# A ninth 2 MB buffer in a two-batch convolution kernel: what it does to loads and stores

## The reference: what is computed

```python
xl1 = _bn_relu(_dwconv(x, w1), g1, b1)          # w1 covers the whole height
xl2 = _bn_relu(_dwconv(x, w2), g2, b2)          # w2 covers the whole width
dot_cb = jnp.einsum('bck,bck->cb', xl1[:, :, 0, :], xl2[:, :, :, 0])
num = dot_cb.reshape(b, c)
num = num @ lw1.T + lb1
num = num @ lw2.T + lb2
num = jax.nn.softmax(num, axis=1)
return x * num[:, :, None, None]                # inside: x is _gn(x); outside: _gn(x) + this
```

## Time and profile before

| | |
|---|---|
| median of 3 runs | 1786.57 us (1786.38 to 1789.39) |
| the profiled execution's own time | 1788.11 us |
| its span | 1786.4 us |
| moved by DMA | 728.07 MB, mean 408 GB/s over the span |
| VectorE busy | 933.8 us (52%) |
| ScalarE busy | 649.6 us (36%) |
| TensorE busy | 484.8 us (27%) |
| GpSimd busy | 318.1 us (18%) |

### The profile page before, as it was taken

How to read it: one execution, slowest core, us unless ns; L and a number is a source line. 1 busy time by engine, 2 the same in 40 slices (tenths; PEclk the granted TensorE clock), 3 DMA queues, 4 the chain that set the end, 5 groups by cost and what they waited for, 6 DMA issues and landing times.

```text
span 1786.4 us, 12512 instructions
## 1 busy us (share of the span) xinstructions
PE 484.8 (27%) x3214; PEld 163.5 (9%) x3214; DVE 933.8 (52%) x4046; ACT 649.6 (36%) x504; POOL 318.1 (18%) x409
## 2 busy tenths in 40 slices
PE   4588566642132322322322233440000000000000
PEld 1132122120000010100100010120000000000000
DVE  5899699933655654555565546963222222222221
ACT  4688587844444544543355345510000000000000
POOL 7678587820000000000000000010000000000000
PEclk8899788865666656656665666765555555555555
DMA  9997899959999999999999999999999999999999
GB/s 387 425 427 304 356 427 427 427 223 419 403 428 401 405 411 409 400 394 430 404 398 405 399 400 431 429 369 413 430 433 430 432 431 431 431 431 431 431 430 409
DMA packets 52425, 728.07 MB, mean 408 GB/s; under 512 B 6273, under 2 KB 6785, under 8 KB 8066
## 3 DMA queue, kind: packets, MB, share of 16 engines
q1 hardware_dynamic: 34210, 463.03, 61.7%
q10 hardware_dynamic: 18144, 264.25, 35.2%
HBM read 458.82 MB, written 268.44 MB: 407 GB/s over the span
## 4 chain that ended last, share of the span: by engine, by line
DMA 53%; another core or an unknown queue 26%; ACT 7%; DVE 6%; PE 4%; SPq 1%; issue 1%; POOL 1%; ACTq 0%; POOLq 0%; DVEq 0%
DMA xs<-in_x 40%; DMA out<-xs 12%; DVE mul_junk L829 4%; ACT sq_junk L650 4%; ACT xs L711 3%; PE ps_part L478 2%; DVE xs L907 1%; DMA z<-in_w 1%; SPq L307 1%; PE ps_l L571 0%; PE ps_m L584 0%; PE ps_l L559 0%; SPq L263 0%; SPq L255 0%
## 5 line engine op out<-in xcount | busy, mean ns | idle before, releaser
L829 DVE SCALAR_TENSOR_TENSOR mul_junk<-xs,ps_w 128x256 bf16<-128x256 f32 x1856 | 643.1, 417 | 317.3 <-DMA xs<-in_x 290.4
L650 ACT ACTIVATE sq_junk<-xs 128x4096 fp8e5<-128x4096 f32 x128 | 463.3, 3619 | 421.7 <-DMA xs<-in_x 405.9
L478 PE MATMUL ps_part<-xs,taps 128*32 128x512 f32 x2048 | 339.8, 824 | 658.2 <-DMA xs<-in_x 658.2
L907 DVE TENSOR_SCALAR xs<-xs,scale,shift 128x4096 f32<-128x4096 f32 x98 | 239.9, 2467 | 409.8 <-DMA xs<-in_x 409.2
L478 PEld LDWEIGHTS ps_part<-xs,taps 128*32 128x32 f32 x2048 | 91.0, 144 | 879.8 <-issue 866.0
L829 DVE DVE_READ_ACCUMULATOR mul_junk<-xs,ps_w 128x1 f32 x1856 | 153.3, 83 | 0.0
L396 POOL TENSOR_TENSOR rstd_b<-var,minus_half 128x2 f32<-128x2 f32 (+1 forms) x16 | 12.4, 774 | 717.8 <-DVE var L856 717.8
L370 POOL TENSOR_TENSOR prod<-xs,w_copy 128x768 f32<-128x768 f32 x64 | 116.4, 1825 | 79.8 <-DMA xs<-in_x 77.5
L711 ACT ACTIVATE xs<-xs,shift,scale 128x4096 f32<-128x4096 f32 x30 | 113.7, 3788 | 14.0 <-DVE scale L940 7.1
L376 POOL TENSOR_TENSOR prod<-prod 128x384 f32<-128x384 f32 x64 | 63.0, 1006 | 0.0
L380 POOL TENSOR_TENSOR prod<-prod 128x192 f32<-128x192 f32 x64 | 36.6, 594 | 0.0
(11 more groups left out here) (100 smaller groups left out, 280.6 us busy)
## 6 DMA issues: line engine op xcount, KB each, us to landing
xs<-in_x SPq DMA_DIRECT2D x216, 2048.0 KB, 19.8
out<-xs ACTq DMA_DIRECT2D x126, 2048.0 KB, 27.1
xs<-in_lw SPq DMA_DIRECT2D x2, 2048.0 KB, 20.8
out<-xs SPq DMA_DIRECT2D x2, 2048.0 KB, 10.9
w_c<-in_w_rows SPq DMA_DIRECT2D x1, 512.0 KB, 4.6
w_sb<-in_w SPq DMA_DIRECT2D x1, 512.0 KB, 9.7
z<-in_w SPq DMA_DIRECT2D x1, 512.0 KB, 23.7
affine_in<-in_g SPq DMA_DIRECT2D x2, 16.0 KB
```

The costliest lines, as they stand in the source:

```text
L478: last = nc.tensor.matmul(ps_part[g % 2][32 * a:32 * a + 32, :], taps[:, g // QG % 2, g % 2, hf * JH + j, :], xs[:, s[0]:s[1] + 1:s[1] - s ...
L650: nc.scalar.activation(sq_junk[:], xs[:, s, :], ACT.Square, accum_out=sq_sum[:, u % 2, u // 2, b:b + 1], saturate=False).then_inc(squared, 1)
L829: last = nc.vector.scalar_tensor_tensor(out=mul_junk[:, sets[0] % 2, j - first, :], in0=xs[:, s, j * W:(j + 1) * W], scalar=1.0, in1=ps_w2 ...
L907: return nc.vector.tensor_scalar(xs[:, s, :], xs[:, s, :], scale[:, b, g:g + 1], shift[:, b, g:g + 1], ALU.mult, ALU.add)
```

## The change

There are nine slots. The room comes from `taps`, which loses its second copy (its halves that hold plain ones are now written anew for the first two groups of every four), and from `mul_junk`, which becomes an 8-bit float tile. The ninth slot, number 8, is used for reloads together with 6 and 7 (`AHEAD = 3`), and at the end it holds one more `b = 1` part for stage 3 (`HELD = 5`), so stage 3 loads 59 parts instead of 60. The ring of three slots lasts to unit 18 instead of 14 (`RING3` 15 to 19).

```diff
-S = 8
+S = 9
-RING3 = 15
+RING3 = 19
 KEPT = 4
+HELD = 5
 REWORK = FIRST - KEPT
-LAST_ORDER = list(range(UNITS - KEPT, UNITS)) + list(range(UNITS - KEPT))
+AHEAD = 3
+LAST_ORDER = list(range(UNITS - HELD, UNITS)) + list(range(UNITS - HELD))
@@ def slot_of(u, b):
-    return 4 + u % 2 + 2 * (u >= UNITS - 2)
+    return 8 if u == UNITS - HELD else 4 + u % 2 + 2 * (u >= UNITS - 2)
 def rework_slot(r):
-    return 6 + r % 2
+    return (8, 6, 7)[r % AHEAD]
 def last_slot(i):
-    return (4 + i) % S
+    return (8 + i) % S if i < 1 or i % S == 0 else (3 + i % S) % 8
@@ tiles
-        taps = sb("taps", [P, 2, 2, JR, 2 * CG])
+        taps = sb("taps", [P, 2, JR, 2 * CG])
-        mul_junk = sb("mul_junk", [P, 2, SET, W], bf16)
+        mul_junk = sb("mul_junk", [P, 2, SET, W], mybir.dt.float8e5)
@@ SyncE
             def load_again(r):
                 s = rework_slot(r)
-                if r < 2:
-                    free_of_statistics(FIRST - 2 + r, 1)
-                else:
-                    sp.wait_ge(x_stored[s], written(s, ("re", r - 2)))
+                if r >= AHEAD:
+                    sp.wait_ge(x_stored[s], written(s, ("re", r - AHEAD)))
+                elif r:
+                    free_of_statistics(FIRST - 3 + r, 1)
...
+            load_again(0)
             load(FIRST, 1)
             load(FIRST + 1, 1)
-            load_again(0)
             load_again(1)
+            load_again(2)
...
-                if u - FIRST + 2 < REWORK:
-                    load_again(u - FIRST + 2)
+                if u - FIRST + AHEAD < REWORK:
+                    load_again(u - FIRST + AHEAD)
-            for i in range(KEPT, UNITS):
+            for i in range(HELD, UNITS):
@@ GpSimd
             def build(g):
                 qp = g // QG % 2
+                if g % QG < 2:
+                    nc.gpsimd.tensor_copy(taps[:, g % 2, :, CG * (1 - qp):CG * (2 - qp)],
+                                          own[:].unsqueeze(1).to_broadcast([P, JR, CG]))
                 nc.gpsimd.tensor_tensor(
-                    taps[:, qp, g % 2, :, CG * qp:CG * (qp + 1)], own[:].unsqueeze(1).to_broadcast([P, JR, CG]),
+                    taps[:, g % 2, :, CG * qp:CG * (qp + 1)], own[:].unsqueeze(1).to_broadcast([P, JR, CG]),
                     bc(w1_sb[:, g, :], CG), ALU.mult).then_inc(taps_ready, 1)
@@ ScalarE
-            rework(0)
-            rework(1)
+            for r in range(AHEAD):
+                rework(r)
...
-                    if b == 0 and u > FIRST and u - FIRST + 1 < REWORK:
-                        rework(u - FIRST + 1)
+                    if b == 0 and u > FIRST and u - FIRST - 1 + AHEAD < REWORK:
+                        rework(u - FIRST - 1 + AHEAD)
@@ VectorE, in multiply_rows
-                            out=mul_junk[:, sets[0] % 2, j - first, :], in0=xs[:, s, j * W:(j + 1) * W], scalar=1.0,
+                            out=mul_junk[:, sets[0] % 2, j - first, :], in0=xs[:, s, j * W:(j + 1) * W], scalar=1.0, saturate=False,
```

More of the change, by code:

```diff
@@ L71 @@
 for _i in range(UNITS):
-    if _i >= KEPT:
+    if _i >= HELD:
         LOADS[last_slot(_i)].append(("last", _i))
@@ L333, in build @@
                 qp = g // QG % 2
+                if g % QG < 2:
+                    nc.gpsimd.tensor_copy(taps[:, g % 2, :, CG * (1 - qp):CG * (2 - qp)],
+                                          own[:].unsqueeze(1).to_broadcast([P, JR, CG]))
                 nc.gpsimd.tensor_tensor(
-                    taps[:, qp, g % 2, :, CG * qp:CG * (qp + 1)], own[:].unsqueeze(1).to_broadcast([P, JR, CG]),
+                    taps[:, g % 2, :, CG * qp:CG * (qp + 1)], own[:].unsqueeze(1).to_broadcast([P, JR, CG]),
                     bc(w1_sb[:, g, :], CG), ALU.mult).then_inc(taps_ready, 1)
-            def plain(qp, i):
-                then_wait(nc.gpsimd.tensor_copy(
-                    taps[:, qp, i, :, CG * (1 - qp):CG * (2 - qp)], own[:].unsqueeze(1).to_broadcast([P, JR, CG])))
-            plain(0, 0)
             pool.wait_ge(w1_loaded, 16)
             build(0)
-            plain(0, 1)
             build(1)
@@ L418, in setup @@
                 if u == 0:
-                    for i in range(2):
-                        plain(1, i)
                     then_wait(nc.gpsimd.memset(minus_half[:], -0.5))
@@ L478, in convolve @@
                     last = nc.tensor.matmul(
-                        ps_part[g % 2][32 * a:32 * a + 32, :], taps[:, g // QG % 2, g % 2, hf * JH + j, :],
+                        ps_part[g % 2][32 * a:32 * a + 32, :], taps[:, g % 2, hf * JH + j, :],
                         xs[:, s[0]:s[1] + 1:s[1] - s[0], j * W:(j + 1) * W],
@@ L972, in _ @@
                 s = last_slot(i)
-                if i >= KEPT:
+                if i >= HELD:
                     dve.wait_ge(x_loaded[s], landed(s, ("last", i)))
```

## The result

The changed kernel takes 1745.93 us (median of 4 runs, 1745.46 to 1746.32) against 1787.98 us (4 runs, 1786.38 to 1789.44) for the kernel before in the same series: a ratio of 0.9765, 95% interval 0.9752 to 0.9777. That is 42.1 us or 2.35% faster. The forecast was 1736 with a range of 1724 to 1760, so the time lies inside the range, 9.9 us above the predicted value.

The account below looks back on a forecast made before the run. DMA transfers at a 431 GB/s ceiling were taken as the bound. Gains of 4.9 + 17.0 + 4.9 + 24 = 50.8 us left 1737.3 of the profiled 1788.1, 1735.8 as median: forecast 1736 us, range 1724 to 1760.

Parts of the forecast that it names:

- The frame: Whole kernel: transfers bound it; stretches below 431 GB/s lose about 99 us of the 1786.4 us span.
- the ring: Stage 1, 155 to 190 us: three slots to unit 18 remove the wait behind the copied bias, gaining 17.0 of 20.6 us.
- the third reload slot and its early reload: Stage 2 and the gap before it: gains of 24 and 4.9 us, 28.9 together.
- One held part more: Stage 3: one load fewer in a saturated stretch, 2.097 MB at 431 GB/s, gaining 4.9 us.
- The rival of the half-closed gap: Stage 1: unit 20's load is as late as the bias was, gain 9.7 instead of 17, 1743 us; chance 0.12.
- The ninth slot between the stages: End of stage 1: the first reload needs no wait and fills 4.9 us of the dead gap of 373 to 393.
- Three reload slots in stage 2: 450 to 1100 us: releases come about one unit earlier, reads do not run dry; 24 of 36.2 us gained, about 422 GB/s.
- The first rival: Stage 2 keeps its rate of 407 as the next wait stops SyncE as long; gain 0 to 10, 1755 us; chance 0.22.
- the full recovery: Stage 2 wins back all 36.2 us instead of 24, 1724 us; chance 0.08.
- End of stage 2: Unit 59's part waits for the last reload's store but is due two units later: unchanged, 0; 8.3 us stay lost.
- Taps and scratch: Extra tap copies on GpSimd and VectorE's 8-bit scratch writes, mainly stage 1: no cost, 0 taken for each.
- The slower rival: Stage 1: slow 8-bit writes make VectorE the bound; 86 ns more per instruction eats the gain; chance 0.03.

Follow-up runs that it names:

- The turned ring: Against the kernel with only unit 59's slot exchanged (1744.22 us): three slots to unit 16, four-slot ring turned from unit 17; 1744.37 us, ratio 0.9739.

## Why the prediction was right, and where it was not

**The frame held.** All of the difference is found as DMA time lost or saved, stretch by stretch, and the sum of the stretches (42.9) meets the difference of the spans (42.5). By the two moments of the section above, the forecast of 17.0 for the ring stands against 14.7, that of 28.9 for the third reload slot and its early reload against 22.4, and that of 4.9 for the held part against 5.4.

**One held part more: 4.9 forecast.** Right in size where its place was full; 4.4 us with two reload slots. With three it brought nothing (1744.01 with four held, 1745.93 with five), since the load that it saves fits into a gap at the end. The prediction counted this transfer "in a saturated stretch"; the time that it frees lies in the gap before it. (On the rate, the Trainium skill, "DMA: Bandwidth & Descriptors", Bandwidth, gives about 358 GB/s to each of two cores of a pair that stream at once and 425 to one that streams alone, so it does not disagree with the 431 of this trace as the prediction had it.)

**The ring: 17.0 forecast, 15.2 by the stretches, 14.4 alone.** The term was right, a little over-sized: 3.6 us were allowed for what remains and 5.5 were lost. The rival of the half-closed gap (9.7) is out. The turned ring shows that the remainder is not the queue's: without the dip the first row-0 scale comes at 376.41 us, 0.4 to 2.6 us before that of the kernels with it. That it is VectorE's (47.66 of 50 us busy) is likely and not tested.

**The ninth slot between the stages: 4.9 forecast, 3.6 by the stretches.** From 340 to 400 us the two kernels without the early reload (ring alone, two reload slots) move 258 GB/s and the changed kernel 292, which is 4.7 us; in its second execution it moves 276, which is 2.5. The mechanism holds, and the size is known to a microsecond or so.

**Three reload slots in stage 2: 24 forecast, 35.9 measured.** The mechanism was right and the size too small. The prediction took two thirds because one of four slow rows lay away from a release. That row (213 GB/s at a share of 0.83) has gone with the others, since the stretch now runs at 430 throughout. The first rival, that the rate stays at 407, is refuted by that rate, though its first half was true: the next wait did come, 194.7 us at L257. What spoke for it, the busy share, misled: 0.98 left 19 us to be had, and 36 were there, so the engines counted as busy in part of the time that was lost. The Trainium skill ("DMA: Bandwidth & Descriptors", Anatomy of one DMA), with its fixed 2.0 us beside the bytes, gave 4 us a round. That section of the Trainium skill gives the cost for transfers issued from GpSimd, and these are issued by SyncE and ScalarE, so it was a guess by likeness. The round lost 2.9 on the mean and now loses next to nothing, so the full recovery that it spoke for came nearer than the two thirds, and its size was too high.

**End of stage 2: the step that failed.** The prediction said of it "it is due two units later. Unchanged, 0". The stretches give a loss of 16.7 us more than before. The argument looked only at when the held part is due, and not at what is left to move while the queue waits. With the two-slot rhythm, 430 GB/s were still moved from 1100 to 1150 us; with three slots, the last reload is stored from 1027.03 on, and from there the queue has nothing but parts whose slots wait for stores. What the runs show of the cause: it is not unit 59's slot (another slot, 362 GB/s), not the order of the last slots (365), not mainly VectorE (366 with a quarter of its work gone there), and only in part the fifth held part (375 without it, 5.6 us of the 16.7). It did not come while stage 2 kept two reload slots: that kernel has 404 GB/s in the same 150 us and 400 from 1050 to 1200, where its stage ends. What stands in the trace is the chain of store, load, statistics, store, with SyncE 84 to 85 us behind stores in every kernel with five held parts and three reload slots. That this chain sets the end is read from the traces and was not shown by a run that shortens it. Keeping back reloads cut the waits, and other slots and less work for VectorE moved the holes, and yet in all the kernels with three reload slots the last unit's square starts between 1121.2 and 1125.8 us, and the first scale of row 1 comes some 34 us behind it, between 1154.8 and 1159.3. That moment, and not the holes as such, sets the time: from it to the end it is 585.3 to 585.7 us in all of them but the two with reloads kept back. What would bring it forward stays open.

**Taps and scratch: 0 forecast.** Right: 0.9996 (0.9971 to 1.0021) for both, and 416 ns for 417. The slower rival (86 ns more) is out.

So the two misses, 11.9 us too little in stage 2 and 16.7 at its end, cancel for the greater part, which is luck and not foresight, and with 1.8 in the ring and 1.3 between the stages the sum comes out 7.9 us short by the stretches (50.8 - 42.9), 9.9 by the medians, of which 1.4 is that the kernel before ran at 1787.98 in this series and not 1786.57.

No version that does all of the work beat the changed kernel by more than some 3 us. The lowest, with earlier slots for the last units, had 1743.48 us against 1746.46 beside it.

## What to carry to other kernels

Where transfers bound a kernel, count the DMA time lost stretch by stretch against the best rate that its own trace shows, and do not read the busy share as what can be won: a share of 0.98 went with 5.6% lost here. When a deeper buffer makes a steady stretch run full, write down what is left to transfer behind it, since slack that the old rhythm left for the end is gone, and a part of the gain comes back as a gap there. A transfer is worth its bytes only if the place where it falls away was full; in a gap it is worth nothing. And ask of a gap whether closing it brings forward the result that the next stage waits for: here four ways of moving the holes about left that moment within 5 us.

## What was unexpected of the hardware

- With loads and stores mixed, the core's DMA engines held 430 GB/s over 620 us of stage 2, beside all the compute, as in stage 3 without it (431). The same mix with reads that ran dry for a moment twice in a round gave 407 to 409 at a busy share of 0.98 to 0.99.
- VectorE writes an 8-bit float result as fast as a bfloat16 one in this form (416 and 417 ns for 128 x 256 from float32).
